# Rounding of the attended values on VectorE, and key stacks in the order even/odd, tile and sequence, on one Trainium2 core

## What is computed

```
tgt1 = layer_norm(x, g1, be1)
q, k, v = tgt1 @ Wq.T + bq, tgt1 @ Wk.T + bk, tgt1 @ Wv.T + bv
p   = softmax(q k.T / sqrt(16) + (1 - mask) * -1e9)      # per head
tgt = x + (p v) @ Wo.T + bo + (memory @ Wg.T + bg)
out = tgt + relu(layer_norm(tgt, g2, be2) @ W1.T + b1) @ W2.T + b2
```

## Time and profile before

| | |
|---|---|
| median of 3 runs | 1938.49 us (1938.28 to 1940.06) |
| profiled execution, its own time | 1938.98 us |
| its span, first to last instruction | 1937.4 us |
| TensorE matmul busy | 1808.3 us, 93% |
| TensorE weight load busy | 1743.6 us, 90% |
| ScalarE busy | 1492.5 us, 77% |
| VectorE busy | 1236.3 us, 64% |
| GpSimd busy | 841.5 us, 43% |
| mean busy share of the 16 DMA engines | about 64%, 222662 packets, 183.69 MB |

### The profile page before, as it was taken

The page is one execution under the profiler, slowest core; times in us unless marked ns, Lnnn a source line. Parts: engine busy times, 40 slices in busy tenths (PEclk is TensorE's granted clock), DMA queues, the critical chain, the costliest instruction groups (busy, mean ns, idle before and its releaser), DMA issues.

```text
span 1937.4 us, 54246 instructions
## 1 busy us (share of the span) xinstructions
PE 1808.3 (93%) x17972; PEld 1743.6 (90%) x17972; DVE 1236.3 (64%) x6745; ACT 1492.5 (77%) x5641; POOL 841.5 (43%) x907
## 2 busy tenths in 40 slices
PE   5799999999999999999999999999999999999997
PEld 4699999999999999999999999999999999999987
DVE  5566666666666666666666666666666666666662
ACT  3787787787787787787787787787787787787782
POOL 2244444444444444444444444444444444444444
PEclk8899999999999999999999999999999999999999
DMA  7765765765765755755756756756756756756740
GB/s 148 93 87 93 111 86 91 113 85 90 115 84 90 112 86 92 110 88 92 110 86 93 110 86 94 109 86 95 110 85 95 107 86 97 105 87 98 100 67 22
DMA packets 222662, 183.69 MB, mean 95 GB/s; under 512 B 14768, under 2 KB 197424, under 8 KB 222384
## 3 DMA queue, kind: packets, MB, share of 16 engines
q1 hardware_dynamic: 222384, 180.23, 63.2%
HBM read 62.73 MB, written 16.78 MB: 41 GB/s over the span
## 4 chain that ended last, share of the span: by engine, by line
PE 58%; ACT 32%; issue 5%; DVE 3%; DMA 1%; SPq 0%; ACTq 0%; POOL 0%; DVEq 0%; POOLq 0%
ACT scores L361 18%; PE ffn_ps L779 8%; PE ffn_ps L781 8%; PE ffn_ps L780 8%; PE turn_ps L842 8%; PE work_ps L779 6%; PE work_ps L781 5%; PE work_ps L780 5%; ACT hid L408 4%; PE value_ps L867 3%; PE score_ps L828 3%; PE work_ps L796 3%; ACT k_hi L434 3%; DVE attnT_lo L564 2%; ACT q_hi L425 2%
## 5 line engine op out<-in xcount | busy, mean ns | idle before, releaser
L361 ACT ACTIVATE scores<-scores,row_min 128x128 f32<-128x128 f32 x2048 | 798.1, 410 | 0.2
L705 POOL TENSOR_TENSOR hT_lo<-hid,hT_hi 128x512 fp32r<-128x512 f32 x256 | 331.1, 1293 | 635.8 <-DVE hT_hi L627 635.8
L371 ACT ACTIVATE probs<-turn_ps 128x512 f32<-128x512 f32 x512 | 307.7, 602 | 309.6 <-PE turn_ps L842 308.2
L599 DVE CUSTOM_DVE_ANT_0 scores<-score_ps,mask_bias 128x128 f32<-128x128 f32 x2048 | 471.5, 286 | 2.9 <-issue 2.7
L361 ACT ACTIVATION_READ_ACCUMULATOR scores<-scores,row_min 128x1 f32 x2048 | 427.8, 209 | 0.0
L842 PE MATMUL turn_ps<-ident,scores 128*128 128x128 f32 x2048 | 310.7, 275 | 2.0 <-ACT probs L371 2.0
L779 PE MATMUL ffn_ps<-zT_hi,w_lo 128*128 128x256 f32 x1024 | 304.7, 298 | 5.6 <-ACT hid L408 4.8
L779 PE MATMUL ffn_ps<-w_hi,hT_lo 128*128 128x256 f32 x1024 | 303.0, 296 | 1.9 <-ACT hid L408 1.9
L781 PE MATMUL ffn_ps<-zT_hi,w_hi 128*128 128x256 f32 x1024 | 290.3, 283 | 0.0
L780 PE MATMUL ffn_ps<-zT_lo,w_hi 128*128 128x256 f32 x1024 | 289.0, 282 | 0.0
L781 PE MATMUL ffn_ps<-w_hi,hT_hi 128*128 128x256 f32 x1024 | 287.4, 281 | 0.0
(11 more groups left out here) (112 smaller groups left out, 4203.7 us busy)
## 6 DMA issues: line engine op xcount, KB each, us to landing
q_stack<-q_hi SPq DMA_DIRECT2D x128, 256.0 KB, 6.9
k_stack<-k_hi SPq DMA_DIRECT2D x256, 128.0 KB, 6.0
x_in<-x_dram SPq DMA_DIRECT2D x64, 256.0 KB, 3.8
mem_in<-memory_dram SPq DMA_DIRECT2D x64, 256.0 KB, 6.7
x_res<-x_dram SPq DMA_DIRECT2D x64, 256.0 KB, 6.9
q_stack<-q_lo SPq DMA_DIRECT2D x64, 256.0 KB, 4.2
k_stack<-k_lo SPq DMA_DIRECT2D x128, 128.0 KB, 5.7
out_dram<-y SPq DMA_DIRECT2D x64, 256.0 KB, 2.1
```

What stands on the lines that cost most here:

```text
L361: last = act.activation(scores[:, k, h, :], scores[:, k, h, :], ACT.Exp, bias=row_min[:, k, h:h + 1], scale=-1.0, accum_out=row_sum[:, k, ...
L371: act.activation(probs[:, k % CPB, :], turn_ps[k % 2][:, :], ACT.Copy).then_inc(probs_copied, 1)
L599: last = dve.tensor_tensor_reduce(out=scores[:, t, h, :], in0=score_ps[t % 2][:, h * S:(h + 1) * S], in1=mask_bias[:, b, :], scale=1.0, sc ...
L705: pool.tensor_tensor(halves[1], src, halves[0], ALU.subtract).then_inc(done, 1)
```

## The change

Two parts.

1. The cast of `attn` into the high part leaves ScalarE's tick 4 and becomes a `tensor_copy` on VectorE at tick 2, right behind the product that makes `attn`. VectorE waits there for its own product (`attn_ready`) and for the projection of the group before (`proj_ready`). The subtraction that makes the low part moves on VectorE from tick 4 to tick 3, behind the cast of the hidden half and ahead of the low part of q.
2. `k_stack` gets the shape `[P, CPB, 2, KT * GB, S]`: even/odd stands outside of tile and sequence. For one partition, one head chunk and one of even/odd, the values are now one run of 512, so that a transfer has rows of 2 KB on both sides. The moving operand of a score matmul becomes two runs of 128 values, 2 KB apart. Bytes, number of transfers and number of matmuls stay.

```diff
-        k_stack = [sb(f"k_stack{n}", [P, CPB, KT * GB, 2, S], F32R) for n in range(2)]
+        k_stack = [sb(f"k_stack{n}", [P, CPB, 2, KT * GB, S], F32R) for n in range(2)]
...
-                            sp.dma_start(k_stack[g % 2][to:to + HD, :, :, e, :]
-                                         .rearrange("p r k s -> p (r k) s").bitcast(F32),
-                                         kk[high_low][HALF * e:HALF * (e + 1)]
-                                         .rearrange("p k (b s) -> p (k b) s", b=GB).bitcast(F32)
+                            sp.dma_start(k_stack[g % 2][to:to + HD, :, e].bitcast(F32),
+                                         kk[high_low][HALF * e:HALF * (e + 1)].bitcast(F32)
                                          ).then_inc(k_stacked, 16)
...
-                    if out_ and t == 4:
-                        g = i - 1
-                        split_high(attn[:], attnT[0], attn_ready, g + 1, proj_ready,
-                                   g if later(g) else None, attnT_hi)
...
                         dve.tensor_tensor(attn[:], value_tiles, inv[:], ALU.mult).then_inc(attn_ready, 1)
+                        dve.wait_ge(attn_ready, g + 1)
+                        if later(g):
+                            dve.wait_ge(proj_ready, g)
+                        dve.tensor_copy(attnT[0][:], attn[:]).then_inc(attnT_hi, 1)
...
-                    if out_ and t == 4:
+                    if out_ and t == 3:
                         split_low(attn[:], attnT, attnT_hi, i, attnT_split)
...
-                                     k_stack[i % 2][:, c, GB * k + b].rearrange("p e s -> p (e s)"),
+                                     k_stack[i % 2][:, c, :, GB * k + b, :],
```

More of the change, by code:

```diff
@@ L677, in _ @@
                 pool.wait_ge(zeros_set, 2 * n + 1)
-                pool.memset(k_stack[n][:].rearrange("p r k e s -> p (r k e s)").bitcast(F32), 0.0
+                pool.memset(k_stack[n][:].rearrange("p r e k s -> p (r e k s)").bitcast(F32), 0.0
                             ).then_inc(zeros_set, 1)
```

## The result

| | before | after |
|---|---|---|
| median | 1938.6 us | 1839.1 us (1836.7 to 1840.5) |
| ratio to before | | 0.948 (95%: 0.947 to 0.950) |
| profiled execution, its own time | 1938.98 us | 1838.27 us |
| span | 1937.4 us | 1836.6 us |
| one iteration in the middle | 29.15 us | 27.55 us |

The account below looks back on a forecast made before the run. TensorE, 93% busy, was taken as the bound, stalled waiting for attention's low part. 1938.98 - 96.1 for the stalls, + 1 for the last one, - 0.5 at the start, - 0.5 to the median gave 1843 us; range 1835 to 1888.

Parts of the forecast that it names:

- The stall's worth: TensorE's wait for attention's low part costs 1.56 us of pace each iteration; 96.1 us in total was taken off.
- The cast at zero cost: VectorE, tick 2: new cast blocked by GpSimd until about 917.1, yet within 1.97 us of idle time; zero cost.
- The subtraction and the race: VectorE, tick 3: subtraction starts before GpSimd's hT_lo, low part 1.4 us early; price zero to 0.1 us.
- Rival A: GpSimd's hT_lo starts first and blocks VectorE's subtraction; TensorE waits about 0.7 us for q; 1886 us, chance 0.11.
- The strided operand: Score matmuls' moving operand in two runs costs TensorE zero; upper bound 129 us.
- rival B: Score matmuls' strided operand runs at half rate on TensorE, adding 129 us; 1972 us, chance 0.03.
- The key transfers: SyncE's key transfers stay hidden before TensorE's scores, 1.1 us left even if 2 KB rows bring nothing.
- Rival C: Key transfers or ScalarE in ticks 5 to 7 become late, 0.5 us each iteration; 1874 us, chance 0.09.

Follow-up runs that it names:

- e4: Changed kernel plus a same-size cast into a spare buffer on ScalarE at tick 4, keeping its load as before; 1839.6 us.
- e3: Changed kernel with the subtraction back at tick 4, behind score chunk 4; 1858.1 us.
- e7: Changed kernel plus three idle statistics instructions on VectorE behind the new cast in each iteration; 1837.2 us.
- e8: Changed kernel plus six idle statistics instructions on VectorE behind the new cast in each iteration; 1882.2 us.
- e5: Changed kernel with the cast back on ScalarE, but at tick 3, so the subtraction starts behind GpSimd's hT_lo; 1889.7 us.
- e2: Kernel before with only part 2, the new key stack order; cast and subtraction where they were; 1933.9 us.
- e1: Changed kernel with the key stacks back in their old order, so only part 1 remains; 1888.1 us.
- e9: e1 with the subtraction behind the low part of q at tick 3, releasing the query transfers earlier; 1855.7 us.
- e6: Changed kernel with the subtraction at tick 3 but behind the low part of q; 1839.0 us.
- e10: Changed kernel plus two more 128 KB transfers in each group, ahead of the keys in the queue; 1940.8 us.

## Why the prediction was right, and where it was not

- **The stall's worth: right.** 1.56 us for each iteration was read, 1.60 (29.15 - 27.55) measured; forecast 1843, measured 1839.1. The sum took 96.1 / 63 = 1.53 us rather than 1.60, about 4 us too little, and the start gained 1.7 us (38.81 for 40.55) rather than 0.5. The chain that I named (attn ready, ScalarE's queue, cast, subtraction, TensorE) is the one: e4 shows that ScalarE's load isn't it, e3 that the subtraction's place is part of it.
- **The cast at zero cost: right, with the upper bound as its price.** I had it blocked and ended at 917.5, 1.3 us behind the product; it was 1.23 us long, and 0.70 us of VectorE's idle time were left, as forecast. e7 and e8 confirm the room behind it.
- **The subtraction and the race: right.** It got in 0.16 us ahead of GpSimd. Rival A's mechanism was real, and its price, 0.7 us, was near the 0.81 of e5.
- **The strided operand (rival B): right at zero.** e2 carries it and is not slower, and its score matmuls are 0.12 us apart, as before.
- **The key transfers: wrong.** The step said that 1.1 us would be left if rows of 2 KB bring nothing, "hidden either way". e1 is that case, and it is 0.79 us late in each iteration. The step took the shift of the keys' issue (1.27 us earlier) as the shift of their landing. But the keys stand in line behind the query transfers, and the same prediction had those released 0.62 us later. The right sum from its own numbers is 1.4 of room (the landings give 1.59 - 0.09 = 1.50 at the median), less 1.56 because TensorE comes earlier, less 0.62 because the line starts later: -0.78 us. Its sentence that the query transfers "are not late for the same reason" had the order backwards: what stands ahead in the queue passes its delay on. e9, which takes the 0.62 away, gave 0.52 of it back. The traces agree: from before to e1 the last key's landing moved 2.18 us against TensorE's first projection matmul, as the first query issue did (2.16), while the first key issue moved 0.28.
- **Why the forecast came out all the same.** This was in part luck: part 2 was priced at zero, with and without it; in truth it pays for what part 1 spends. Its rows of 2 KB took 1.5 us out of the line, and 0.7 to 0.8 us of slack were left. The sum was right for a kernel with both parts, and would have been 45 us off for part 1 alone. Rival C named the place (the key transfers) and put its threshold at 1.1 us; it was 0.7 to 0.8 with the new rows and already passed without them.

## What to carry to other kernels

When a stall on the bound engine goes, everything that was only just in time for it is due earlier by the whole stall. Transfers issued one behind the other are counted from the first in their line, not from their own issue. An edit that brings almost nothing by itself (here 2 to 5 us alone) can be what lets another one have its gain, so measure the parts of a change apart and together. Where VectorE and GpSimd both read SBUF, look which of the two starts first, and put a held-up instruction where its engine is idle.

## What the runs showed of the hardware

- SBUF to SBUF transfers, three of 256 KB (queries) and six of 128 KB into 16 partitions each (keys): from the first issue to the last landing 16.4 us with key rows of 512 bytes and 14.9 with rows of 2 KB. The issues don't make the difference: SyncE's six take 3.30 us from first to last in e1 and 3.18 in the changed kernel. The page counts 148934 packets for 222662, and the difference, 73728, is 64 groups of 1536 rows less 384, so a row is a packet. I had taken it as open whether the length of a row tells at all. The Trainium skill, page "DMA: Bandwidth & Descriptors", section "Why small descriptors are slow (HBM only)", says that SBUF to SBUF transfers don't suffer the penalty of small descriptors. At 512 bytes against 2 KB these kernels show a difference, and the measurement decides.
- One more transfer of 128 KB in this line, with rows of 2 KB, made it 1.0 to 1.2 us longer.
- A VectorE subtraction with two SBUF inputs that starts while GpSimd works on SBUF tiles took 0.5 to 0.7 us longer (1.22 in e6, 1.35 in e5, for 0.69), and a cast from SBUF to SBUF 0.8 us longer (1.23 for 0.43). GpSimd, in its turn, took 1.68 us for 1.29 when the subtraction had started first.
- A wait for a DMA's landing mostly appears in these traces as "issue": at TensorE in e1 and e10, where each first score of groups 8 to 59 starts 0.09 us behind a landing.
